# First node product of a two-layer graph network: GpSimd only gathers, its two normalised tiles go to VectorE and ScalarE

## The reference, cut to what matters

```python
h = relu(layernorm(x))                       # (50000, 128)
# layer 1 of L0: s1 = h @ sl1  + per edge  h[src] @ w1[type], summed at dst
x1 = relu(segment_sum(einsum('nd,rde->rne', h, w1)[type, src], dst) + h @ sl1 + b1)
# layer 2 of L0: the same with x1, w2, sl2, b2
# then x + result, another layernorm and relu, and the message-passing layer L1
```

## Time and profile before

| | |
|---|---|
| median of 3 runs | 2980.29 us (2977.81 to 2980.57) |
| the profiled execution's own time | 2981.61 us |
| its span in the profile | 2979.9 us |
| PE busy | 2220.2 us (75%) |
| DVE busy | 2123.9 us (71%) |
| ACT busy | 1569.0 us (53%) |
| POOL busy | 2117.5 us (71%) |
| granted TensorE clock, mean | 0.916 |

### The profile page before, as it was taken

The page is one execution under the profiler, slowest core; times in us unless marked ns, Lnnn a source line. Parts: engine busy times, 40 slices in busy tenths (PEclk is TensorE's granted clock), DMA queues, the critical chain, the costliest instruction groups (busy, mean ns, idle before and its releaser), DMA issues. The chain is left out here.

```text
span 2979.9 us, 56436 instructions
## 1 busy us (share of the span) xinstructions
PE 2220.2 (75%) x16219; PEld 1900.0 (64%) x16219; DVE 2123.9 (71%) x7295; ACT 1569.0 (53%) x3333; POOL 2117.5 (71%) x1577
## 2 busy tenths in 40 slices
PE   4779988888768898888845666577777777566765
PEld 4769888888667898888844565344444444354554
DVE  6978777677423586667627776677777777499999
ACT  4986555555423354444426776344444444476774
POOL 6775888888667288888857774688887777455555
PEclk9999999999889999999977888898999889799998
DMA  6985555555379645554529998444444443465663
GB/s 217 306 276 123 108 101 102 101 101 104 55 270 349 228 87 86 85 86 86 86 25 386 411 408 338 107 93 86 91 85 86 87 86 58 134 200 190 193 197 132
DMA packets 268196, 473.22 MB, mean 159 GB/s; under 512 B 62736, under 2 KB 142288, under 8 KB 268112
## 3 DMA queue, kind: packets, MB, share of 16 engines
q1 hardware_dynamic: 158352, 382.24, 38.8%
q0 software_dynamic: 109760, 90.00, 20.0%
HBM read 291.28 MB, written 180.81 MB: 158 GB/s over the span
## 5 line engine op out<-in xcount | busy, mean ns | idle before, releaser
L1149 POOL DMA_INDIRECT s<-E_summed,c_scat x392 | 658.8, 1681 | 207.3 <-issue 113.4
L1377 PE MATMUL ps<-c_w,E_masked 128*128 128x128 f32 x6272 | 738.0, 280 | 3.5 <-DVE E_masked L1180 3.4
L1377 PEld LDWEIGHTS ps<-c_w,E_masked 128*128 128x128 f32 x6272 | 730.0, 197 | 4.3 <-DVE E_masked L1180 4.3
L1180 DVE SCALAR_TENSOR_TENSOR E_masked<-E_type_row,E_hT 128x512 f32<-128x512 int32 x784 | 483.5, 687 | 79.9 <-ACT E_hT L1297 67.0
L366 POOL DMA_INDIRECT E_src_rows<-s,c_src x392 | 417.7, 1065 | 166.4 <-issue 118.0
L1487 POOL DMA_INDIRECT s<-E_summed,c_scat x196 | 322.5, 1646 | 100.6 <-issue 55.5
L1476 POOL DMA_INDIRECT E_ends<-x,c_near x196 | 199.9, 1020 | 95.2 <-issue 58.5
L1328 ACT COPY E_summed<-ps 128x512 f32<-128x512 f32 x98 | 57.4, 586 | 398.9 <-DMA s<-E_summed,c_scat 398.9
L366 POOL DMA_INDIRECT E_src_rows<-in_x,c_src x196 | 202.4, 1033 | 75.3 <-issue 60.3
L586 PE MATMUL ps<-c_sl,N_hT 128*128 128x128 f32 x1568 | 198.0, 281 | 18.4 <-DVE N_out L407 13.8
L1392 PE MATMUL ps<-E_msg,E_same 128*128 128x128 bf16 (+1 forms) x2450 | 207.3, 241 | 1.2 <-DVE E_msg L1230 1.2
(11 more groups left out here) (143 smaller groups left out, 4854.6 us busy)
## 6 DMA issues: line engine op xcount, KB each, us to landing
s<-N_out SPq DMA_DIRECT2D x147, 512.0 KB, 4.7
N_xin<-in_x SPq DMA_DIRECT2D x98, 512.0 KB, 5.5
N_sin<-s SPq DMA_DIRECT2D x98, 512.0 KB, 5.6
E_dst_row<-in_dst_line SPq DMA_DIRECT2D x147, 256.0 KB, 4.8
E_type_row<-in_type SPq DMA_DIRECT2D x98, 256.0 KB, 3.9
N_xin<-s SPq DMA_DIRECT2D x49, 512.0 KB, 6.4
x<-N_x SPq DMA_DIRECT2D x49, 512.0 KB, 11.6
N_xin<-x SPq DMA_DIRECT2D x49, 512.0 KB, 4.1
```

Source lines behind the costliest of these rows:

```text
L1149: pool.indirect_dma_start(s, bass.IndirectOffsetOnAxis(ap=c["scat"][:, k:k + 1], axis=0), summed[:, g % 2, t * D:(t + 1) * D], None, compu ...
L1180: nc.vector.scalar_tensor_tensor(out=masked[:, u % 2, r, :], in0=type_row[:, u, :], scalar=float(r), in1=hT[:, u % 2, :], op0=ALU.is_equal ...
L1377: ins = nc.tensor.matmul(ps[:, 2 + u % 2, t * D:(t + 1) * D], masked[:, u % 2, r, t * P:(t + 1) * P], w[:, r, :], start=(r == 0 and t == 0 ...
```

## The change: what it does

GpSimd normalises nothing any more in the first node product. Tile 3 goes to VectorE, which now has tiles 0 to 3, and tile 4 to ScalarE, which has 4 to 7. The semaphore `pool_normed` and its waits on TensorE and VectorE go. GpSimd issues its gathers of that stage in one run, and twice as many: 144 (36 groups) in place of 72. The first edge pass issues 2 gathers a group in place of 3; as 52 are left in place of 124, they are out after 26 groups, where they were after 42.

```diff
-N0_AHEAD = 18
+N0_AHEAD = 36
@@ node_product
-    ON_ACT, ON_POOL = 3, 2
-    ON_DVE = NT - ON_ACT - ON_POOL
+    ON_ACT = 4
+    ON_DVE = NT - ON_ACT
@@ GpSimd
-            if not norm:
-                gathers.issue(pool, x, GT * N1_AHEAD)
-                return
-            gathers.issue(pool, x, 3 * GT)
-            for g in range(GROUPS_N):
-                u = g % UNROLL
-
-                pool.wait_ge(ln.rstd_ready, g + 1)
-                for k in range(ON_DVE, ON_DVE + ON_POOL):
-                    tile = xin[:, u, k * D:(k + 1) * D]
-                    ins = ln.normalise(nc.gpsimd, tile, tile, k, u)
-                ins.then_inc(pool_normed, 1)
-                gathers.issue(pool, x, 3 * GT + (N0_AHEAD - 3) * GT * (g + 1) // GROUPS_N)
+            gathers.issue(pool, x, GT * (N0_AHEAD if norm else N1_AHEAD))
@@ VectorE
                 wait(dve, act_normed, g - 3)
-                wait(dve, pool_normed, g - 3)
@@ TensorE
                     pe.wait_ge(normed, g + 1)
-                    pe.wait_ge(pool_normed, g + 1)
                     pe.wait_ge(act_normed, g + 1)
@@ edge_pass_relational, GpSimd
-                gathers.issue(pool, x, gathers.issued + (3 if norm else 2))
+                gathers.issue(pool, x, gathers.issued + 2)
```

More of the change, by code:

```diff
@@ L392, in node_product @@
     if norm:
-        normed, act_normed, pool_normed = S("normed"), S("act_normed"), S("pool_normed")
+        normed, act_normed = S("normed"), S("act_normed")
     turned, hT_ready, product, out_ready = S("turned"), S("hT_ready"), S("product"), S("out_ready")
```

## The result

The changed kernel took **2963.97 us** (median of 4 runs, 2961.72 to 2965.21) against 2980.43 before in the same comparison: a ratio of 0.994, 95% interval 0.9922 to 0.9958. That is 16.5 us faster. The forecast was 51 us, 2929, with a range up to 2951. The direction was right and the size wrong by a factor of three.

A forecast was written before the change was run, and what follows sets the result against it. GpSimd's scatters and gathers were taken to bound the first edge pass, VectorE and ScalarE the first node product. -61 us and +10 us made -51 us on 2981.6, so 2929 us for the median, range 2908 to 2951.

The forecast's parts named there:

- GpSimd's period with three gathers, 12.11 us: First edge pass before the change: four scatters (8.08 us) and three gathers (4.03 us) with their gaps make a group's time.
- the rule for copy k: First edge pass: ScalarE's copy k of the sums comes 13.1 + (k - 2) x period after copy 0.
- Two gathers with their gaps take 2.69 us, so the third gather is all cost and the first two are nearly free: First edge pass: two gathers nearly cover the 2.81 us landing wait; dropping the third brings the period to 10.75 us.
- The check by the second edge pass: That pass has the same pattern of four scatters and two gathers; its sum, 10.72 us, supported the 10.75 us period.
- No gathers from group 26 on: First edge pass: four scatters plus the bare landing wait, 10.4 us a group, 218.4 us for 21 groups.
- The forecast of 500.3 us for the 48 intervals: First edge pass: 281.9 us with gathers plus 218.4 us without, in place of 561.6, so -61 us.
- The gathers are covered by the node product: First node product: 144 gathers take 183 to 194 us, the stage 199 us, so they cost nothing on GpSimd.
- Their cost on the DMA engines: First node product: later-landing loads lengthen the period by at most 0.67 us, 0 to +32 us over 48 groups.
- The two tiles: First node product: fourth tiles on ScalarE and VectorE give a period of 3.95 us, +10 us with later loads inside.
- TensorE taking over: Rival 2: first edge pass period stays near 11.2 us because of TensorE, 2957 us in all; chance 0.13.
- Rival 3: The first node product pays nothing (+2 us) and edge-pass groups without gathers take 9.83 us: 2908 us; chance 0.15.
- rival 4: The gathers do not fit under the first node product, which ends slower: +50 us, 3030 us; chance 0.05.

The follow-up runs named there:

- before_late: The kernel before, three gathers a group, with only SyncE's row loads of the first edge pass made to wait for landed scatters: 2974.4 us against 2978.93, ratio 0.9991.
- late_loads: The changed kernel, but in the first edge pass SyncE's row loads and source-row store wait until an earlier group's scatters have landed: 2923.87 us, ratio to before 0.9816.
- tiles_only: The kernel before with only the two normalised tiles moved, as many gathers as before, those of the node product in one run: 2969.98 us, ratio 0.9972.

## Why the prediction was wrong, by its steps

*GpSimd's period with three gathers, 12.11 us, and the rule for copy k*: right; before_late shows it again.

*"Two gathers with their gaps take 2.69 us, so the third gather is all cost and the first two are nearly free"*: this step failed. It priced the landing wait at 2.81 us from the earlier trace rows and took it to stay as it was. For the kernel before that was right even in the middle of the pass: the landing came 1.84 us behind the last scatter's issue, and GpSimd starts 0.8 us behind a landing, 2.6 us in all, which two gathers cover. But without the third gather the scatters move up against SyncE's 768 KB, which then starts 3.84 us behind the first scatter in place of 2.13; the landing comes 2.97 us behind the last one, 3.8 us with GpSimd's start, and two gathers with their gaps are 2.6 to 2.7. GpSimd's waits rise from 0.15 to 1.14 us a group, so that taking the gather away gave 12.11 - 11.45 = 0.66 us a group, not 1.36. The check by the second edge pass did not find this: that pass runs with two gathers and hardly waits, and it has no store of source rows and does not release its loads by VectorE's scatter rows. Which of the two spares it, no run tells.

*"No gathers from group 26 on", 10.4 us*: failed by the same term, a landing wait of 4.0 us in place of 2.81. With the loads out of the way (late_loads) the period is 10.02; in the changed kernel it was 11.6. I put the faster last groups of the pass down to VectorE running out of work; for the most part it was the loads that ran out, since late_loads has 10.0 us in the middle of the pass with VectorE busy 105 of 120 us. For the last two intervals, 9.6 to 9.8 us in both kernels, VectorE is not ruled out.

The forecast of 500.3 us for the 48 intervals is within 3 us of late_loads's 497.1, in part by luck: its first 27 intervals took 287.1 us (forecast 281.9) and the other 21 took 210.1 (forecast 218.4). GpSimd's part of the period with gathers was sized about right, 10.75 against 10.98; the term left out was SyncE's traffic beside the last two scatters.

*The gathers are covered by the node product*: right. They follow one another in steps of 1.27 us and the last ends at 200.8 us, 24 us before the stage. *Their cost on the DMA engines*: bounded by 0 and 32 us, measured about 8 (6 to 9.5, tiles_only). *The two tiles*: the period was forecast at 3.95 us and is 120 / (270 / 9) = 4.0, and from the first transpose to the last copy the stage grew by 11.2 us, so the +10 was right in size. But I had worked it out from the tiles, with the later loads inside, and by tiles_only 3 of the 11 us are the tiles' and 8 the gathers'. That the size fits is in part luck. What I left out is the start of the stage, where GpSimd's tiles stood behind 12 gathers: -4.7 us. The sum for the stage was +10 and is +6.4 in this pair of profiles. VectorE's tile is also shorter without GpSimd's beside it, 0.347 us in the place of 0.410. The Trainium skill, SBUF — State Buffer, section "SBUF: two separate sides", has VectorE and GpSimd hold a shared port pair in turns; the shorter tile agrees with it, while the other half of that rule, that four tiles on VectorE would hold up the gathers, is not borne out: they took 0.965 us each. The prediction also had the trace agree for the instruction with two SBUF inputs; for that kind the same section has contention only against a GpSimd operation that reads SBUF, and it gives the descriptor lock for the 2-port modes alone, so the 1.85 us of the earlier trace rows is a row of its own and no support for the lock.

*The rivals*: TensorE taking over (11.2 us, 2957 us) is nearest in time and wrong in cause; TensorE's share hardly rose, and the period fell to 10.0 when only SyncE's transfers moved. Rival 3 had the node product free, which it is not, and rival 4 did not come. No rival had a transfer of another queue as the thing uncovered. The rows for one stood in the trace: ScalarE waited for scatters to land in every group, the DMA share was 0.52, and the 6.03 us at 763.51 stood right above the 2.81 us that I took.

## What to carry to other kernels

When an instruction is taken away in front of a wait, the wait need not keep the length that it had in the old trace. Ask what else is timed from the same event. Here one landing released the scatters directly and another queue's transfers 4.6 us later, and the instruction that was removed had held the scatters back; without it the transfers fell on the last two of them. So place the other queues' transfers on the new timeline before pricing the wait, and look for a stretch of the old trace where they already meet it (here the wait of 6.03 us). Where a chain hangs on the landing of the last small transfer, keep other queues' bulk transfers out of that moment: one added wait that moves them can be worth more than the work removed, here 40 us against 16.5.

## What was not expected of the hardware

Between 657.3 and 659.5 us, 223 packets of SyncE's queue filled the 16 DMA engines to 98% and none of GpSimd's began, though the issue of its scatter had ended at 656.79. The mean wait in front of a run of scatters was 4.0 us with these transfers beside the last two, and 2.55 us with the same bytes moved in front of the first two.
